# Attention batches with their pieces reordered, the expert choice by single operations over two batches, positions on GpSimd, and expert registers read once a round

## The reference: what is computed

```python
x = x + _L0_attn_a_ref(_layernorm(x), ...)   # S4D: a long convolution, then a layer norm
x = x + _L0_ffn_ref(_layernorm(x), ...)      # mixture of experts
x = x + _L0_attn_b_ref(_layernorm(x), Wqkv, Wout)
x = x + _L0_ffn_ref(_layernorm(x), ...)      # the same mixture, same weights

def _L0_attn_b_ref(x, Wqkv, Wout):           # 16 heads of 8, causal, with a slope per head
    q, k, v = jnp.split(x @ Wqkv, 3, axis=-1)
    logits = jnp.einsum('bihd,bjhd->bhij', q, k) * scale + slopes * rel
    logits = jnp.where(causal, logits, -jnp.inf)
    return jnp.einsum('bhij,bjhd->bihd', softmax(logits), v) @ Wout

def _L0_ffn_ref(x, gate_w, gate_b, w1, b1, w2, b2, ws1, bs1, ws2, bs2):
    top_w, top_i = jax.lax.top_k(x @ gate_w + gate_b, 2)      # 2 of 8 experts for each row
    combine = one-hot of top_i weighted by softmax(top_w)
    out = sum over e of combine[:, e] * (gelu(x @ w1[e] + b1[e]) @ w2[e] + b2[e])
    return out + gelu(x @ ws1 + bs1) @ ws2 + bs2              # and a shared expert
```

## Time and profile before

| | us |
|---|---|
| time, median of 3 runs (lowest, highest) | 892.42 (891.72, 892.74) |
| time of the profiled execution | 891.84 |
| its span | 889.8 |
| busy in the span: PE, DVE, ACT, POOL | 632.5, 627.4, 444.7, 456.5 |
| granted TensorE clock, mean of the span | 0.872 of full speed |

### The profile page before, as it was taken

The page is one execution under the profiler, slowest core; times in us unless marked ns, Lnnn a source line. Parts: engine busy times, 40 slices in busy tenths (PEclk is TensorE's granted clock), DMA queues, the critical chain, the costliest instruction groups (busy, mean ns, idle before and its releaser), DMA issues. The chain is left out here.

```text
span 889.8 us, 21991 instructions
## 1 busy us (share of the span) xinstructions
PE 632.5 (71%) x7826; PEld 469.5 (53%) x7826; DVE 627.4 (71%) x1407; ACT 444.7 (50%) x873; POOL 456.5 (51%) x569
## 2 busy tenths in 40 slices
PE   0559964860099999035899998998954795999950
PEld 0354433650088998023566665665632574998950
DVE  6997987781068888377777778778643872888856
ACT  5535366740055556253657665755633332555534
POOL 1138858887547777310011312564564881677760
PEclk9958996995599999655899999999976897999995
DMA  9510003341144443522122232333011412455518
GB/s 286 138 37 1 0 7 74 68 90 51 45 78 88 89 97 76 184 68 67 49 57 75 70 92 55 110 81 93 25 38 32 82 36 47 84 98 100 91 26 281
DMA packets 131850, 70.51 MB, mean 79 GB/s; under 512 B 89535, under 2 KB 118725, under 8 KB 131746
## 3 DMA queue, kind: packets, MB, share of 16 engines
q1 hardware_dynamic: 121042, 50.46, 23.9%
q0 software_dynamic: 9088, 16.88, 6.8%
q10 hardware_dynamic: 1616, 1.77, 0.7%
HBM read 26.61 MB, written 30.50 MB: 64 GB/s over the span
## 5 line engine op out<-in xcount | busy, mean ns | idle before, releaser
L1451 ACT ACTIVATE ARENA<-banks,ARENA 128x256 f32<-128x256 f32 x312 | 122.1, 475 | 104.1 <-PE banks L1414 84.3
L2164 DVE TENSOR_REDUCE ARENA<-banks 128x4 f32<-128x1024 f32 (+1 forms) x128 | 122.7, 958 | 47.2 <-PE banks L1905 46.0
L1412 PE MATMUL banks<-ARENA,W1H 128*128 128x256 f16 x312 | 87.0, 279 | 66.2 <-DMA ARENA<-slots 58.8
L2086 ACT ACTIVATE ARENA<-banks 128x1536 f32<-128x1536 f32 x64 | 92.8, 1450 | 59.2 <-PE banks L1933 59.2
L1426 PE MATMUL banks<-W2L,ARENA 128*128 x624 | 110.7, 219 | 2.8 <-DVE ARENA L1464 2.3
L1428 PE MATMUL banks<-W2H,ARENA 128*128 x624 | 110.0, 219 | 0.0
L1427 PE MATMUL banks<-W2H,ARENA 128*128 x624 | 110.0, 219 | 0.0
L1402 POOL DMA_INDIRECT expert_out_g<-ARENA x78 | 80.0, 1026 | 48.1 <-issue 25.7
L1402 POOL DMA_INDIRECT expert_out_f<-ARENA x78 | 80.7, 1034 | 36.9 <-issue 25.4
L1485 DVE TENSOR_TENSOR ARENA<-ARENA 128x1024 f16<-128x1024 f32 x78 | 95.6, 1225 | 2.7
L1014 POOL DMA_INDIRECT slots<-ARENA,PLACE x64 | 77.7, 1214 | 28.4 <-issue 20.4
(11 more groups left out here) (312 smaller groups left out, 1783.9 us busy)
## 6 DMA issues: line engine op xcount, KB each, us to landing
spread<-ARENA SPq DMA_DIRECT2D x96, 64.0 KB, 2.0
ARENA<-expert_out_f SPq DMA_DIRECT2D x8, 512.0 KB, 7.5
ARENA<-spread SPq DMA_DIRECT2D x16, 256.0 KB, 3.1
ARENA<-spread SPq DMA_DIRECT2D x32, 128.0 KB, 3.0
ARENA<-expert_out_g SPq DMA_DIRECT2D x8, 512.0 KB, 7.4
XT<-in_w SPq DMA_DIRECT2D x10, 256.0 KB, 7.7
slots<-EMPTY SPq DMA_DIRECT2D x16, 129.0 KB, 4.6
ARENA<-in_w SPq DMA_DIRECT2D x8, 256.0 KB, 6.8
```

The lines of the kernel that those rows point to most:

```text
L1412: pe.matmul(out, t.W1H[:, e, ms], XST[i][:, 0], start=True, stop=False)
L1451: ins = nc.scalar.activation(HF[i % 2][:, m], UP[i % 2][:, m], ACT.Gelu, bias=BIAS[i % 4][:, m:m + 1], scale=1.0 / WS)
L2086: nc.scalar.activation(PR[x % 2], t.psum_all[:, 5:8, :], ACT.Exp, scale=1.0 / LOGIT).then_inc(exps, 1)
L2164: dve.tensor_reduce(MX[:, G // 2, tile, :, :, G % 2].rearrange("p s a -> p a s"), src, AX.X, ALU.max).then_inc(m_red, 1)
```

## The change

PE's pieces of a quarter are put on both sides of `maxima(x+5, 1)`, `values` moves from G2 to the end of G1, `turn_maxima(b+1, 0)` from G1 to G2, and `gate` and `rank` from G2 to G3; ACT follows in its order. On DVE each piece gets a place after the first or after the second reduction; `split(b+3)` moves from G0 to G1, `add` from G1 to G2, statistics of a batch from G2 of batch c+2 to G0 of batch c+3 (the last two excepted). For groups 0 and 1 the choice is one chain of eleven single operations, spread over the quarters from G3 of the gate's batch to G2 of the batch after next, `rank` comes two batches after the gate instead of one, and the products of `place` run on GpSimd; group 2 keeps the old way. SP does both spreads before the transposes. GpSimd's `rows(c)` follow `statistics(c)` of the same c, and a group's 16 scatters are issued as 4, 8 and 4 in c = 4g+7, 4g+8 and 4g+9. In the routed stages `EID` is a single list; PE and DVE read the first 8 entries at the start and each later round's in the middle of the round before.

```diff
-    flat = t.EID.rearrange("p k r u -> p k (r u)")
-    dve.tensor_copy(flat[:, 0, 0:SLOTS], EIDF)
-    dve.tensor_copy(flat[:, 1, 2:SLOTS], EIDF[:, 0:SLOTS - 2])
-    dve.tensor_copy(flat[:, 2, 0:SLOTS - 2], EIDF[:, 2:SLOTS]).then_inc(listed, 1)
+    dve.tensor_copy(t.EID.rearrange("p r u -> p (r u)")[:, 0:SLOTS], EIDF).then_inc(listed, 1)
...
+    def place_on_pool(pool, g):
+        pool.wait_ge(ranks_read, g - part.first + 1)
+        tt = nc.gpsimd.tensor_tensor
+        for k in range(2):
+            ins = tt(VV[:, k], O12[:, k], POS, ALU.mult)
+        link_pool(pool, ins)
+        for width in (NE // 2, NE // 4):
+            link_pool(pool, tt(VV[:, :, :, 0:width], VV[:, :, :, 0:width], VV[:, :, :, width:2 * width], ALU.add))
+        link_pool(pool, tt(PK.rearrange("p k (t o) -> p k t o", o=1), VV[:, :, :, 0:1], VV[:, :, :, 1:2], ALU.add))
+        nc.gpsimd.tensor_copy(t.PLACE[:, :, GRP * g:GRP * g + GRP], PK).then_inc(placed, 1)
...
         def body(k, first, last):                      # PE, routed
-            mine = expert_values(pe, k, 0)
-            late = expert_values(pe, k, 1)
             for i in range(tiles_of(last)):
-                up(k, i, mine[i])
-                if not (first and i < 2):
-                    down(k, i - 2, late[i])
+                n = k * UN + i
+                up(k, i, experts[n])
+                if n >= 2:
+                    down(k, i - 2, experts[n - 2])
+                if i == UN // 2 and not last:
+                    experts.extend(expert_values(pe, k + 1))
...
                 if batch(b + 1):                       # SP
                     spread_m(b + 1, 0)
+                    spread_m(b + 1, 1)
                 if 0 <= b - 3 < NB - 1:
                     batches.turn(sp, b - 3)
-                if batch(b + 1):
-                    spread_m(b + 1, 1)
...
                 batches.statistics(pool, c)            # GpSimd
-                if c >= 1:
-                    batches.rows(pool, c - 1)
                 for g in range(SENT_IN_ATTENTION):
-                    piece = c - 4 * g - 6
-                    if piece in (0, 1):
-                        route.dispatch_first(pool, g, range(GRP // 2 * piece, GRP // 2 * piece + GRP // 2))
-                    if piece in (2, 3):
-                        route.dispatch_second(pool, g, (piece - 2,))
-            batches.rows(pool, NB - 2)
+                    if c == 4 * g + 7:
+                        route.place_on_pool(pool, g)
+                batches.rows(pool, c)
+                for g in range(SENT_IN_ATTENTION):
+                    if c == 4 * g + 7:
+                        route.dispatch_first(pool, g, range(0, GRP // 2))
+                    if c == 4 * g + 8:
+                        route.dispatch_first(pool, g, range(GRP // 2, GRP))
+                        route.dispatch_second(pool, g, (0,))
+                    if c == 4 * g + 9:
+                        route.dispatch_second(pool, g, (1,))
...
+                if G == 0 and batch(b - 2):            # PE, between scores and maxima(x + 5, 1)
+                    turn_out(b - 2)
+                if G == 1 and batch(b - 2):
+                    project_out(b - 2)
+                if G == 2 and batch(b + 1):
+                    pe.wait_ge(vset, b + 2)
+                    turn_maxima(b + 1, 0)
+                if G == 3: (gate or rank, after mrow_set)
                 if quarter(x + 5):
                     maxima(x + 5, 1)
+                if G == 0 and batch(b + 3):
+                    project(b + 3)
+                if G == 2 and batch(b - 1):
+                    turn_back(b - 1, 0)
...
                 if quarter(x - 1):
                     weigh(x - 1)
+                if G == 1 and batch(b + 1):
+                    values(b + 1)
...
+                if G == 2 and batch(b + 1):            # ACT: values and scalar(b - 3) ahead of expo(x)
+                    values(b + 1)
                 if G == 2 and 0 <= b - 3 < NB - 1:
                     batches.scalar(act, b - 3)
                 if quarter(x):
                     expo(x)
...
                 if quarter(x + 4):                     # DVE, one of the eight places
                     reduce(x + 4, 0)
+                if G == 0:
+                    if 0 <= b - 3 < NB - 2:
+                        statistics(b - 3)
+                    if first_step is not None:
+                        route.choose_step(dve, first_step, 1)
+                    if second_step is not None:
+                        route.choose_step(dve, second_step, 6)
+                    if last is not None:
+                        route.second(dve, last)
```

More of the change, by code:

```diff
@@ L923, in route_program @@
     part = Bag()
-    part.steps = 0
+    part.steps = part.pool_steps = 0
     def link(dve, ins):
@@ L995, in positions @@
         dve.wait_ge(rank_mm, g - part.first + 1)
+        if g > part.first:
+            dve.wait_ge(placed, g - part.first)
         base = t.BASE[:, g, :]
@@ L1485, in body @@
                 dve.tensor_tensor(H16[i % 4][:, 1], HF[i % 2], H16[i % 4][:, 0], ALU.subtract).then_inc(split, 1)
-                if not (last and i >= tiles_of(last) - 2):
-                    fetch_bias(i + 2, ahead[i])
-                if not (first and i < 2):
-                    take_out(k, i - 2, late[i])
+                if n + 2 < SLOTS:
+                    fetch_bias(i + 2, experts[n + 2])
+                if n >= 2:
+                    take_out(k, i - 2, experts[n - 2])
+                if i == UN // 2 and not last:
+                    experts.extend(expert_values(dve, k + 1))
             if last:
                 for i in range(tiles_of(last) - 2, tiles_of(last)):
-                    take_out(k, i, mine[i])
+                    take_out(k, i, experts[k * UN + i])
         rounds(dve, body)
@@ L1766, in rank_group, with last_rank @@
         def rank_group(b):
-            return gate_group(b - 1)
+            early = gate_group(b - 2)
+            return early if early is not None and early < SENT_IN_ATTENTION else last_rank(b)
+        def last_rank(b):
+            late = gate_group(b - 1)
+            return late if late is not None and late >= SENT_IN_ATTENTION else None
         @block.sync
@@ L1870, in values @@
             def values(c):
-                after(pe, mrow_set, 2 * c + 1)
+                after(pe, parts, min(c + 3, NB))
                 for tile in range(TPB):
@@ L2228, in quarter_of @@
                         normalise(b - 1, 1)
-                    if gate_group(b) is not None:
-                        route.largest(dve, gate_group(b))
-                    if rank_group(b) is not None:
-                        route.place(dve, rank_group(b))
+                    if gated is not None:
+                        if gated < SENT_IN_ATTENTION:
+                            route.choose_step(dve, gated, 0)
+                        else:
+                            route.largest(dve, gated)
+                    if last is not None:
+                        route.place(dve, last)
                 if b == -1 and G == 0:
```

142 lines of the change are left out of this document (87 added, 55 removed).

## The result

The changed kernel takes 882.45 us, the median of four runs (881.04 to 886.28), against 892.07 for the kernel before. The ratio is 0.9899, with a 95% interval of 0.9864 to 0.9934: about 1% faster, 9.6 us where 4.8 was forecast. The profiled execution took 883.78 us, 8.1 less than that of the kernel before; its span is 882.0.

A forecast was written before the change was run, and what follows sets the result against it. PE was taken to bound the attention batches, busy 13.50 of 13.76 us. -9.0 - 2.0 + 8.6 - 2.4 = -4.8 from 891.84 gives 887.0, 887.6 for the median; range 881.5 to 896.5, the forecast's own 884.5 to 890.5.

The forecast's parts named there:

- rival of a tail that is not charged: End of attention: rows do not wait behind POOL's issues or the next block hides it, the 8.6 fall away; 879.0, chance .10.
- E1 to E15: Attention batches b1 to b14, between the exponentials opening b1 and b15: -9.0 us, with the new stall in b12 counted.
- filling: Batches b = -1 and 0: DVE's split, which waits .79 for ACT ahead of the statistics, moves a quarter later; -2.0 us (0 to -3).
- tail: From E15 to the next block: later statistics and POOL's queue in order delay the last transposes; +8.6 us (7 to 10), charged in full.
- expert registers, two stages: Routed stages: 8 loads mid-round; 1.03 lost at each of four boundaries a stage, gain capped at 3.3 to 3.5; -2.4 us taken.
- Choice in single operations: DVE in attention: eleven chained operations spread over slots between reductions; costed at nothing, 5.5 us for two groups if uncovered.
- Pieces of a quarter: PE and ACT in attention: reordered short and long pieces, PE's work unchanged; 13.7 us a batch, between 13.5 and 13.9.
- The wait for SP: SP's queue in attention: with both spreads before the transposes, the store ends at 9.1 of the next batch, 1.3 ahead of 10.4.
- The stall in b12: Attention: ACT's scalar(9) waits for POOL behind eight issues, delaying b12's third exponential; a new stall of .9 us (0 to 2).
- rival of a steady loss by SP's queue: Attention: at the largest transposes and stores the first spread comes .5 late in 13 batches; +6.5, 894.1, chance .16.
- POOL's issues: Attention: rival that DVE operations hold up POOL's indirect DMAs, 1.9 instead of 1.27 each; 901.5, chance .05.
- The cap: Routed stages: POOL's two issues a tile also take 2.65 us, so the register gain is not 8.2 but at most 3.3, 3.5.

The follow-up runs named there:

- regs_only: The kernel before with nothing but the register change (expert registers loaded once a round); 885.46 us, ratio 0.9928.
- blocks: The changed kernel with the choice of groups 0 and 1 again in blocks of five and six operations, two batches apart; 887.57 us against 892.54 before.
- after: The changed kernel itself, as profiled: 883.78 us, span 882.0; median 882.45 us, ratio 0.9899.
- place_dve_sp: The changed kernel with the products of place back on DVE and SP's transposes back between the two spreads; its one run took 886.75 us.
- early: The changed kernel with the choice of groups 0 and 1 in one batch, rank one batch after the gate, scatters four by four from c = 4g+6; 879.66 us, 0.9860.
- undo_regs: The changed kernel with the expert registers as they were (three lists, 16 to 24 registers at each round's start); 891.85 us, ratio 0.9989.
- regs_dve_two: The changed kernel, but DVE loads two sets of 8 registers (three in the last round) at each round's start, all used; 910.87 us, ratio 1.021.
- regs_pe_two: The changed kernel, but PE loads twice 8 registers at each round's start, both used, the second set from a shifted place; 903.66 us, ratio 1.0134.
- after_again: The changed kernel unaltered, run and profiled once more; 883.11 us, ratio 0.9899.
- regs_dve_start: The changed kernel with 16 more DVE register loads meant at each round's start; being unused they were left out, so it equals the changed kernel; 885.4 us.
- the three early ones: Changed kernel with one-batch choice: scatters four by four (879.66 us), last four of group 1 behind the last rows (882.3), or as 4, 8, 4 from c = 4g+6 (880.12).
- early3: As early, with the scatters of a group as 4, 8 and 4 in c = 4g+6 to 4g+8; 880.12 us against 891.56 before.

## Why the prediction was right or wrong, step by step

The measured time lies in the range, near its lower end, and the sign is right. But 882.45 is below the 884.5 to 890.5 given for the forecast itself; it lies where the rival of a tail that is not charged was put (877 to 883), and the tail was charged. So the mechanism was right in attention and wrong in the routed stages, and the gain forecast is half of the one measured. The terms, from the two profiled executions:

| term | predicted | measured |
|---|---|---|
| E1 to E15 | -9.0 | -8.3 |
| filling | -2.0 | -1.5 (-0.8 to -3.4 in twelve profiles) |
| tail | +8.6 | +9.4 |
| expert registers, two stages | -2.4 | -6.0 (-4.3 in regs_only) |
| the rest (front, shared stage, start of g) | 0 | -1.3 |
| span (terms rounded) | -4.8 | -7.8 |

*Choice in single operations: right that it costs nothing, too much in what it was blamed for.* b8 and b12 show no trace of it, and no wait before the maxima is over .6 us, where under 1 was forecast. In the old order of the pieces the blame was nearly right: PE's waits in b8 of before are .94 and 1.37 behind the two blocks, .48 before rank, behind ACT, and PE is busy .4 more, together 3.2 of the 3.1 by which b8 stood out.

```profile
539.39 0.34 PE L1889 MATMUL banks<-ARENA 64*128 64x256 bf16 x4 [0.94 <-DVE ARENA L2164]
549.49 0.21 PE L953 MATMUL banks<-ARENA,BEFORE 128*128 128x72 f16 x1 [0.48 <-ACT ARENA L2075]
```

But in the new order the same blocks cost only .4 to 1.0 each (blocks). The remainder of 5.8 us lies with what moved beside them, the pieces' order, gate and rank no longer behind ACT's copy, and SP's near misses, which no run here divides.

*Pieces of a quarter: inside the range, but not a gain.* An undisturbed batch takes 13.83, inside 13.5 to 13.9; forecast was 13.7, .06 less than before, and it is .07 more, with PE busy 13.59 instead of 13.50. The order pays in the batches that were disturbed.

*The wait for SP: right that it goes, wrong that the order does it.* It is gone in after, but place_dve_sp has the old order and no such wait. The rival of a steady loss by SP's queue doesn't occur: no wait of PE between E1 and E15 ends with a DMA.

*The stall in b12: right in mechanism, worth nothing.* ACT's scalar waits for POOL and the third exponential starts at E12 + 8.1, as forecast:

```profile
595.73 0.88 ACT L1134 ACTIVATE XN<-RES,NRM 128x128 f32<-128x128 f32 x2 [1.15 <-POOL NRM L1121]
596.51 1.43 ACT L2138 ACTIVATE ARENA<-banks 128x1536 f32<-128x1536 f32 x1
598.98 1.45 ACT L2138 ACTIVATE ARENA<-banks 128x1536 f32<-128x1536 f32 x1 [0.31 <-PE banks L1990]
```

The fourth starts at E12 + 10.55, .2 behind b8's (10.38), and the batch takes 13.83. The slack was larger than the .9 that I allowed. (The sum there gives 8.2 + .9 - 6.8 - .9 = 1.4 and not .9; neither was lost.)

*The tail: right, and it eats the batches' gain.* The written-out chain gave rows(14) at 32.95; they end at 32.3. The sum was .8 short because the growth was taken between the transposes' ends, where it is POOL's last work that counts: the block opens 10.6 us behind the last rows in before, after and early, with the drain of 9.04 in between. That ACT's idle time would be no longer than 5 us contradicted the sum itself, which has ACT done at 31.65 and the block, 6.7 behind transposes that end at 35.5, at 42.2; it is 11.79. early shows the mechanism: 4.9 us less on POOL, 4.9 us less to the next block.

*Filling: near the forecast, but one profile does not decide it.* The twelve profiles with the changed attention code take 71.4 to 74.0, and which of these it is goes with the granted clock before E1 (last section).

*POOL's issues: no sign of the rival.* In the change's batches an issue takes .95 to 1.10, as before. b9 takes the same time with the products of place on either engine. The Trainium skill, "SBUF — State Buffer", "Who interferes with whom", says that a DVE operation with two inputs in SBUF contends with GpSimd's reads; no row of these batches shows a cost of that. In the shared stage the rival's condition is met: in after as in before 15 of the 32 issues take 1.5 to 2.9 us, each beside one of the DVE operations over 128x2048 (L1271 and L1273 of before), and the batches have none of that size. (The 9.1 that the rival gives the tail does not follow from the terms it names: twelve issues at .63 more make 7.6.)

*Expert registers: the step that failed.* The cap is what failed: "POOL's two issues a tile also take 2.65" is true and was read as POOL's own rate. POOL's own is 2 x (.98 + .30) = 2.56, and its last three pairs of each stage, before and after, are 2.56 to 2.58 apart. 2.65 is PE's tile, and POOL follows it: when PE loses .9 at a boundary, POOL's next pair is spaced 3.5 to 3.9 us in g, part of it hidden in records of 1.6 to 1.7 us that look like work, and next to nothing is caught up afterwards. The chain of waits ends in POOL because its last issue is the last event of the stage. The right view was PE's group of first products in the stretch of one stage: 3.5 us idle, twice, is 7 us, and all but .4 a stage goes. I had the price of a boundary (1.03) and the number of boundaries (8), and discarded their product, 8.2, for a cap that no wait of PE supported; measured are 6.0, in regs_only 4.3.

Taken by parts, the forecast had -2.4 for attention (-9.0 - 2.0 + 8.6) and -2.4 for the registers. By themselves attention is worth between -2.1 and 0 (undo_regs, 0.9976 to 1.0001 of 892), the registers -6.6 (regs_only): most of the gain is the smaller edit's, and the remaining 2 us come only with both.

## What to carry to other kernels

An engine at the end of the chain with the same pitch as the engine ahead of it is not a second bound; ask which of them idles at the irregular place, in the groups of that stretch alone. Work taken off a busy engine and given, later, to an idle one is paid for where the program drains: write the idle engine's queue out to the end of the stage, and look for what the queue itself still does there (here a drain of 9.04 us behind POOL's last item). And register loads in the queue of the bounding engine are worth spacing out: here .6 to .7 us of them are covered at a boundary, so one load of .75 is as good as free and of two in a row most of the second is paid.

## What the runs showed of the hardware that was not expected

*What a register load takes depends on which entries it reads.* Eight entries that fill a row of the list take .59 to .60 us in most loads (up to .76 for the second of a pair, up to .85 for an engine's first). Seven from the start of a row take 1.05 to 1.22 (last rounds of after and of the experiments). Five from a shifted start take 1.2 to 1.3, eight from a start shifted by two or six entries 1.9 to 2.2 (regs_dve_two and regs_pe_two above). Whether the place, the number or the full row decides was not tried; the start alone does not. The Trainium skill, "DMA: Bandwidth & Descriptors", "Latency and other measured facts", states a floor of about 600 ns for a `tensor_load`; the loads of a full row agree, the others go beyond it by .4 to 1.6 us.

*Two levels at the start of routed g.* Profiles whose code is equal there differ by 2 us between the shared stage's last scatter and the first scatter of g: 20.2 in after, 22.5 in early. PE starts there at half clock. Windows of 2 us in after, in early and in after_again (second number PE busy, the one behind the last bracket the granted clock):

```profile
740.76:742.76 2.00, 1.33 (x7) 0.97 (x8) 0.00 (x0) 0.00 (x0) 0.00 (x0) 0.50 0.37 65
742.76:744.76 2.00, 2.00 (x11) 1.44 (x10) 0.00 (x0) 0.49 (x2) 0.00 (x0) 0.50 0.51 74
744.76:746.76 2.00, 1.79 (x17) 1.32 (x15) 0.85 (x2) 1.86 (x6) 0.00 (x0) 0.98 0.10 5
```
```profile
736.23:738.23 2.00, 1.25 (x7) 0.89 (x8) 0.00 (x0) 0.00 (x0) 0.00 (x0) 0.50 0.37 66
738.23:740.23 2.00, 1.48 (x7) 0.75 (x5) 0.00 (x0) 0.41 (x2) 0.00 (x0) 0.50 0.45 73
740.23:742.23 2.00, 1.11 (x6) 0.81 (x7) 0.78 (x2) 1.16 (x4) 0.00 (x0) 0.50 0.15 7
742.23:744.23 2.00, 2.00 (x11) 1.45 (x10) 1.22 (x2) 0.27 (x1) 0.00 (x0) 0.50 0.37 67
744.23:746.23 2.00, 2.00 (x27) 1.79 (x26) 0.67 (x1) 1.87 (x6) 0.00 (x0) 0.93 0.37 67
```
```profile
740.98:742.98 2.00, 1.25 (x7) 0.89 (x8) 0.00 (x0) 0.00 (x0) 0.00 (x0) 0.50 0.36 64
742.98:744.98 2.00, 1.49 (x7) 0.75 (x5) 0.00 (x0) 0.41 (x2) 0.00 (x0) 0.50 0.48 76
744.98:746.98 2.00, 1.37 (x13) 1.23 (x14) 0.78 (x2) 1.15 (x4) 0.00 (x0) 1.00 0.14 12
```

The clock goes from 0.50 (1.2 GHz) to full (2.4 GHz) 12.1 us behind the shared stage's last scatter in after and 16.3 in early. All 14 profiles divide so: in nine the clock is full by 12.0 to 13.6 us and the first scatter of g comes at 20.2 to 21.2; in five (regs_dve_start, place_dve_sp and the three early ones) it is full at 16.3 to 17.1 and the scatter comes at 22.3 to 22.5. So 2 us between two executions can come from here. It is the larger part of why early's profiled span (880.5) is only 1.5 under the change's (882.0) although its tail is 4.9 shorter. What decides between the levels is open: in early PE has gaps before the rise and in after hardly any, but after_again has early's gaps, window by window, and the full clock as soon as after.

*The same two levels before E1.* The windows of the last 10 us before E1, in blocks, after and early3, have a mean granted clock of 1.00, .83 and .66, a mixture of the two levels; filling takes 71.4, 73.3 and 74.0:

```profile
422.19:432.19 10.00, 7.62 (x120) 4.78 (x113) 6.24 (x10) 7.95 (x17) 0.00 (x0) 1.00 0.12 34
425.02:435.02 10.00, 8.15 (x100) 4.96 (x100) 5.32 (x8) 6.70 (x12) 0.00 (x0) 0.83 0.07 18
425.10:435.10 10.00, 9.21 (x100) 5.53 (x100) 5.47 (x8) 5.67 (x11) 0.00 (x0) 0.66 0.05 15
```

Each of the twelve profiles of the changed attention code has one of these three means, and filling goes with it: 71.4 at 1.00 (two), 72.8 to 73.3 at .83 (seven), 73.8 to 74.0 at .66 (three). The kernel before has .83 there and takes 74.8, so at an equal clock the change wins 1.5 to 2.0. Both places together make up to 5 us between executions of equal code, as much as the four times of the changed kernel differ (881.0 to 886.3; their mean granted clocks fall from .872 and .873 to .866 in that order). The levels of executions without a profile are not known.
